# Value blocks split by ScalarE and TensorE, and twelve tiles' moments moved into the first attention part, in a two-layer gated cross-attention kernel

## The reference, cut to what matters

```python
x = x + tanh(g_xattn[0]) * L0_xattn(layernorm(x), ctx, ...)   # the change is in and before this layer
x = x + tanh(g_ffn[0])   * L0_ffn(layernorm(x), ...)          # 4-bit blocks of 16
x = x + tanh(g_xattn[1]) * L1_xattn(layernorm(x), ctx, ...)
x = x + tanh(g_ffn[1])   * L1_ffn(layernorm(x), ...)          # 8 experts, 2 per token

# inside L0_xattn: 16 heads of 16, 77 context rows per batch
q = (x @ Wq + bq);  k = (y @ Wk + bk);  v = (y @ Wv + bv)
out = softmax(q @ k.T / 4) @ v          # per head
return relu(out @ W1 + b1) @ W2 + b2
```

## Time and profile before

| what | value |
|---|---|
| median of 3 runs | 754.19 us (751.41 to 754.39) |
| the profiled execution, its own time | 754.52 us |
| its span, first to last instruction | 752.8 us |
| PE, DVE, ACT, POOL busy, share of the span | 79%, 73%, 47%, 33% |
| first stage, up to barrier 1 | 0 to about 46 us: DVE 36.4 of 47 us busy, PE 22.6 |
| first attention part | about 46 to 147 us: PE 92.4 of 99 us busy, DVE 78.3, POOL 69.5, ACT 64.6 |

### The profile page before, as it was taken

One profiled execution on the slowest core, in us unless ns is written; L12 is line 12 of the kernel. 1 busy time (PEld: TensorE's weight loads), 2 busy tenths in 40 slices (PEclk: granted clock), 3 DMA queues, 4 the chain that ended last, 5 costly groups with the idle time before them and its releaser, 6 DMA issues. The chain is left out here.

```text
span 752.8 us, 15996 instructions
## 1 busy us (share of the span) xinstructions
PE 595.1 (79%) x5555; PEld 531.4 (71%) x5555; DVE 550.4 (73%) x1173; ACT 351.3 (47%) x873; POOL 250.6 (33%) x253
## 2 busy tenths in 40 slices
PE   4559999799524888888885699998681899999950
PEld 3239999699522777777784599997581689999940
DVE  5958898568996699999974478887558675545437
ACT  2256776523125444444432565655255455565620
POOL 2436777700200000000001266666200475555520
PEclk9999999989955899999997899999755899999985
DMA  8020000030000000000000000000195122222229
GB/s 230 2 64 1 3 2 3 2 116 0 1 0 0 1 1 0 0 0 0 0 0 1 1 2 2 2 3 2 40 374 202 50 84 79 78 77 77 68 75 303
DMA packets 27631, 36.66 MB, mean 49 GB/s; under 512 B 4024, under 2 KB 22265, under 8 KB 27438
## 3 DMA queue, kind: packets, MB, share of 16 engines
q1 hardware_dynamic: 23822, 25.56, 10.5%
q0 software_dynamic: 3744, 10.23, 4.3%
HBM read 26.47 MB, written 9.31 MB: 48 GB/s over the span
## 5 line engine op out<-in xcount | busy, mean ns | idle before, releaser
L948 POOL TENSOR_TENSOR rstd<-mv,eps_col 128x16 f32<-128x16 f32 (+2 forms) x6 | 1.3, 210 | 277.6 <-DVE mv L472 277.6
L978 POOL TENSOR_TENSOR p_lo<-prob,p_hi 128x616 f16<-128x616 f32 x64 | 87.2, 1362 | 5.1
L972 POOL CAST p_hi<-prob 128x616 f16<-128x616 f32 x64 | 44.6, 697 | 68.5 <-ACT prob L1101 68.5
L1029 POOL DMA_INDIRECT y_rows<-rn,dst_row x39 | 43.2, 1108 | 54.4 <-DVE rn L897 53.1
L1101 ACT ACTIVATE prob<-prob 128x616 f32<-128x616 f32 x64 | 46.0, 718 | 32.4 <-DVE prob L575 32.3
L1109 ACT ACTIVATE pT<-ps 128x512 f32<-128x512 f32 (+1 forms) x96 | 46.8, 522 | 26.9 <-PE ps L1440 26.5
L575 DVE TENSOR_TENSOR prob<-ps,smax 128x308 f32<-128x308 f32 x128 | 55.3, 474 | 2.2
L1025 POOL DMA_INDIRECT xin<-x_rows,src_row x39 | 38.3, 982 | 52.6 <-DVE dst_row L864 41.0
L461 DVE CAST ehT_hi<-ehid 128x512 fp32r<-128x512 f32 x39 | 16.6, 426 | 52.9 <-ACT ehid L1331 52.8
L570 DVE TENSOR_REDUCE smax<-ps 128x8 f32<-128x616 f32 x64 | 50.6, 790 | 0.2 <-PE ps L1356 0.2
L1354 PE MATMUL ps<-wgu_hi,fxT_hi 128*128 128x352 f32 x128 | 45.0, 352 | 7.1 <-ACT fxT_lo L1215 7.1
(11 more groups left out here) (282 smaller groups left out, 2037.8 us busy)
## 6 DMA issues: line engine op xcount, KB each, us to landing
el_w<-in_L_ffn_W_dram SPq DMA_DIRECT2D x16, 512.0 KB, 9.9
eh_w<-y_rows SPq DMA_DIRECT2D x16, 256.0 KB, 6.0
x_sb<-in_x_dram SPq DMA_DIRECT2D x4, 512.0 KB, 8.5
x_rows<-rn SPq DMA_DIRECT2D x4, 512.0 KB, 9.8
out_dram<-x_sb SPq DMA_DIRECT2D x16, 128.0 KB, 3.5
stage<-in_L_xattn_W_dram SPq DMA_DIRECT2D x2, 512.0 KB, 3.9
eb<-in_L_ffn_b_dram SPq DMA_DIRECT2D x1, 1024.0 KB, 10.3
w<-in_L_ffn_w_down_dram SPq DMA_DIRECT2D x1, 704.0 KB, 7.5
```

Source lines behind the costliest of these rows:

```text
L972: pool.tensor_copy(p_hi[:, t % 2, c], prob[:, t % 2, c]).then_inc(s["hi"], 1)
L978: pool.tensor_tensor(p_lo[:, t % 2, c], prob[:, t % 2, c], p_hi[:, t % 2, c], ALU.subtract).then_inc(s["lo"], 1)
L1029: pool.indirect_dma_start(y_rows, bass.IndirectOffsetOnAxis(ap=dst_row[:, j:j + 1], axis=0), ey[:, j % YRING], None) .then_inc(y_out[j % Y ...
```

## The change

In the first stage the four value blocks are no longer split by DVE. ACT copies the block from PSUM to 16 bits, PE subtracts that copy from the block where it stands in PSUM (a matmul with a negative 16-bit identity `less_h`, without starting a new sum), ACT copies the rest to 16 bits, PE subtracts again, ACT makes the third part. ACT does the first part of all four blocks, then the high parts of the three weight matrices, then the second and third parts. Three of the four small constants are loaded behind the keys' data, the fourth is gone; three semaphores of x become one. POOL waits for both halves of layer 1's keys before it spreads them, and takes over two of the three low weight parts.

Only tiles 0 to 3 have their moments taken in the first stage. DVE takes those of tiles 4 to 7, 8 to 11 and 12 to 15, with their aggregation, at the end of its steps -2, 1 and 5 of the first attention part. POOL makes inverse deviations and shifts of four tiles at a time (`early_rows`): group 0 in the first stage, group 1 ahead of the MLP's first weight, groups 2 and 3 inside `both_halves` at the top of t = 1 and t = 5. ACT's `normalise` of each pair waits for its group.

```diff
+SOON = 4
+LATER = (-2, 1, 5)
@@ SP
-            sp.dma_start(ident[:, :], I["c_ident"]).then_inc(ld["const"], 16)
-            sp.dma_start(head_mask[:, :, :], I["c_head"]...).then_inc(ld["const"], 16)
-            sp.dma_start(k_mask[:, :], I["c_kmask"]).then_inc(ld["const"], 16)
-            sp.dma_start(stage_sel[:, :], I["c_sel"]).then_inc(ld["const"], 16)
             sp.dma_start(ctxT[:, :, :], ...).then_inc(ld["ctx"], 16)
...
             sp.dma_start(bk_col[:, :], I["L0_xattn_bk_cols"]).then_inc(ld["k"], 16)
+            sp.dma_start(k_mask[:, :], I["c_kmask"]).then_inc(ld["const"], 16)
+            sp.dma_start(ident[:, :], I["c_ident"]).then_inc(ld["const"], 16)
+            sp.dma_start(head_mask[:, :, :], I["c_head"]...).then_inc(ld["const"], 16)
...
-                sp.dma_start(x_sb[:, 4 * c:4 * c + 4], ...).then_inc(ld[f"x{c}"], 16)
+                sp.dma_start(x_sb[:, 4 * c:4 * c + 4], ...).then_inc(ld["x1" if c else "x0"], 16)
@@ DVE, first stage
-            for n in range(2):
-                for b in range(B):
-                    g = 2 * n + b
-                    dve.wait_ge(kp["v_ready"], g + 1)
-                    v = ps[0:M, V_BANK[g], 0:D]
-                    ch.link(dve.tensor_copy(v3[:, g, 0], v))
-                    ch.link(dve.tensor_tensor(v_rest[:, 0], v, v3[:, g, 0], ALU.subtract))
-                    ch.link(dve.tensor_copy(v3[:, g, 1], v_rest[:, 0]))
-                    ch.link(dve.tensor_tensor(v_rest[:, 1], v_rest[:, 0], v3[:, g, 1], ALU.subtract))
-                    dve.tensor_copy(v3[:, g, 2], v_rest[:, 1]).then_inc(kp["v3_ready"], 1)
...
-                    if at < TILES:
-                        if at % 4 == 0:
-                            dve.wait_ge(ld[f"x{at // 4}"], 16)
+                    if at < SOON:
+                        if at == 0:
+                            dve.wait_ge(ld["x0"], 16)
                         moments(at)
-                    elif at == TILES:
-                        aggregate(0)
+                    elif at == SOON:
+                        aggregate(0, last=SOON)
...
-            for n, (hi, lo, at) in enumerate(splits):
-                dve.wait_ge(act_done, n + 1)
-                ch.done(dve.tensor_tensor(lo, stage[:, at], two_parts(hi), ALU.subtract))
+            hi, lo, at = splits[0]
+            dve.wait_ge(act_done, 1)
+            ch.done(dve.tensor_tensor(lo, stage[:, at], two_parts(hi), ALU.subtract))
@@ DVE, attention
                     step(k)
...
+                    if n == 0 and k in LATER:
+                        g = LATER.index(k) + 1
+                        dve.wait_ge(ld["x1"], 48)
+                        for t in range(SOON * g, SOON * (g + 1)):
+                            moments(t)
+                        aggregate(0, first=SOON * g, last=SOON * (g + 1))
@@ POOL
+            def shift_rows(k, n, part, first=0, last=TILES):
...
+            def early_rows(g):
+                inverse_deviation(0, g + 1, first=SOON * g, last=SOON * (g + 1))
+                shift_rows(0, 0, 2 * g + 1, first=SOON * g, last=SOON * (g + 1))
+
+            pool.wait_ge(kp["kT_ready"], 2)
             for hf in range(2):
-                pool.wait_ge(kp["kT_ready"], hf + 1)
                 for b in range(B):
                     for hi in (True, False):
                         spread_keys(pool, 1, hf, b, hi)
-            inverse_deviation(0)
-            shift_rows(0, 0, 1)
+            early_rows(0)
+            for n, (hi, lo, at) in enumerate(splits):
+                if n:
+                    pool.wait_ge(act_done, n + 1)
+                    pool.tensor_tensor(lo, stage[:, at], two_parts(hi), ALU.subtract)
             barrier(pool, 1)
...
             def both_halves(n):
                 for t in range(TILES):
+                    if n == 0 and t in (1, 5):
+                        early_rows(2 + t // 5)
                     if t:
                         low_half(n, t - 1, 1)
                     high_half(n, t, 0)
...
+            early_rows(1)
             mlp_weights(0, w1_hi, w1_lo)
@@ ACT
+            act.wait_ge(ld["const"], 48)
+            act.activation(ident_h[:, :], ident[:, :], ACT.Copy)
+            act.activation(neg_ident[:, :], ident[:, :], ACT.Copy, scale=-1.0)
+            act.activation(less_h[:, :], ident[:, :], ACT.Copy, scale=-1.0).then_inc(kp["less"], 1)
             act.wait_ge(ld["v"], 64)
             act.activation(spread[:, :], ...).then_inc(kp["spread"], 1)
+            for g in range(2 * B):
+                act.wait_ge(kp["v_ready"], g + 1)
+                act.activation(v3[:, g, 0], ps[0:M, V_BANK[g], 0:D], ACT.Copy).then_inc(kp["cast"], 1)
             act.wait_ge(ld["q"], 64)
             for hi, _, at in splits:
                 act.activation(hi, stage[:, at], ACT.Copy).then_inc(act_done, 1)
-            act.wait_ge(ld["const"], 64)
-            act.activation(ident_h[:, :], ident[:, :], ACT.Copy)
-            act.activation(neg_ident[:, :], ident[:, :], ACT.Copy, scale=-1.0)
+            for part in range(1, 3):
+                for g in range(2 * B):
+                    act.wait_ge(kp["rest"], 2 * B * (part - 1) + g + 1)
+                    act.activation(v3[:, g, part], ps[0:M, V_BANK[g], 0:D], ACT.Copy)\
+                        .then_inc(kp["cast"] if part == 1 else kp["v3_ready"], 1)
...
                 def normalise(p):
                     att_wait(act, n, "xt", p)
+                    if n == 0:
+                        act.wait_ge(rs[0], 2 * (2 * p // SOON + 1))
...
-                act.wait_ge(rs[2 * n], 2 + n)
+                if n:
+                    act.wait_ge(rs[2], 3)
@@ PE, behind the value matmuls
+            pe.wait_ge(kp["less"], 1)
+            for part in range(2):
+                for g in range(2 * B):
+                    pe.wait_ge(kp["cast"], 2 * B * part + g + 1)
+                    pe.matmul(ps[0:M, V_BANK[g], 0:D], less_h[0:M, 0:M], v3[:, g, part], start=False, stop=True, skip_group_check=True)\
+                        .then_inc(kp["rest"], 1)
```

More of the change, by code:

```diff
@@ L298, in build @@
         ld = {n: sem(f"ld_{n}") for n in
-              "const x0 x1 x2 x3 ctx k v q w1 w2 bias gu up d wg rank eb".split()}
+              "const x0 x1 ctx k v q w1 w2 bias gu up d wg rank eb".split()}
         stored = sem("stored")
@@ L307, in build @@
         dve_done, pool_done, act_done = sem("dve_done"), sem("pool_done"), sem("act_done")
-        kp = sems("kp", "k_ready k_used kT_ready v_ready b_ready b_used v3_ready c_ready c_used zero spread")
+        kp = sems("kp", "k_ready k_used kT_ready v_ready b_ready b_used v3_ready c_ready c_used zero spread less cast rest")
         tanh_ready = sem("tanh_ready")
@@ L327, in build @@
         rt = sems("r", "const xn xt full logit logits_out gates prob both rank spread picked rows meta")
-        mo = sems("e", "hi weights low xt xhi xlo up h ht bias relu split down y acc")
+        mo = sems("e", "hi weights xt xhi xlo up h ht bias relu split down y acc")
         block = ctx.enter_context(nc.Block())
@@ L394, in _ @@
             for c in range(4):
-                sp.dma_start(x_sb[:, 4 * c:4 * c + 4], xt[:, 4 * c:4 * c + 4]).then_inc(ld[f"x{c}"], 16)
+                sp.dma_start(x_sb[:, 4 * c:4 * c + 4], xt[:, 4 * c:4 * c + 4]).then_inc(ld["x1" if c else "x0"], 16)
             sp.dma_start(gates[:, 0:2], I["g_xattn"].rearrange("(a n) -> a n", a=1).broadcast_to([P, 2])).then_inc(ld["bias"], 16)
@@ L949, in inverse_deviation @@
                 pool.tensor_tensor(r, r, eps_col[:, TILES + first:TILES + last], ALU.pow).then_inc(rs[n], 1)
-            pool.wait_ge(ld["const"], 64)
+            pool.wait_ge(ld["const"], 48)
+            def shift_rows(k, n, part, first=0, last=TILES):
+                pool.wait_ge(rs[n], part)
+                ch.link(pool.tensor_tensor(shift_a[:, k, first:last], mv[:, n, first:last, 0], rstd[:, n, first:last], ALU.mult))
+                pool.tensor_scalar(shift_a[:, k, first:last], shift_a[:, k, first:last], -1.0, None, ALU.mult).then_inc(rs[n], 1)
+            def early_rows(g):
+                inverse_deviation(0, g + 1, first=SOON * g, last=SOON * (g + 1))
+                shift_rows(0, 0, 2 * g + 1, first=SOON * g, last=SOON * (g + 1))
+            pool.wait_ge(kp["kT_ready"], 2)
             for hf in range(2):
-                pool.wait_ge(kp["kT_ready"], hf + 1)
                 for b in range(B):
@@ L956, in _ @@
                         spread_keys(pool, 1, hf, b, hi)
-            def shift_rows(k, n, part):
-                pool.wait_ge(rs[n], part)
-                ch.link(pool.tensor_tensor(shift_a[:, k], mv[:, n, :, 0], rstd[:, n], ALU.mult))
-                pool.tensor_scalar(shift_a[:, k], shift_a[:, k], -1.0, None, ALU.mult).then_inc(rs[n], 1)
-            inverse_deviation(0)
-            shift_rows(0, 0, 1)
+            early_rows(0)
[3 more added lines that the diff above has]
+                    pool.tensor_tensor(lo, stage[:, at], two_parts(hi), ALU.subtract)
```

7 lines of the change are left out of this document (3 added, 4 removed).

## The result

The change makes the kernel **slower by 4.9 us**: the median of 13 runs is 757.83 us (755.79 to 762.20) against 752.91 for 13 runs of before (751.41 to 755.82), a ratio of 1.0062 with a 95% interval of 1.0040 to 1.0085. The forecast of 763 us had the direction right and was 5 us too high; the time lies inside the range, near its low end. The profiled execution took 756.03 us, its span is 754.1.

The account below looks back on a forecast made before the run. Engine handoffs (PE, DVE, ACT, POOL) were taken to bound the first stage, PE attention; -6.8 first stage, +5.8 and +6.0 waits, +3.6 clock make +8.6 us on 754.52, so 763 us, range 757 to 767.

Parts of the forecast that it names:

- first stage: Up to barrier 1: earlier loads, new value split and shorter DVE tail together gain 6.8 us, bounds 4.7 and 7.3.
- first wait (tile 0): Attention, top of t = 1: POOL holds for group 2 ahead of tile 0's second low half; PE loses 5.8 us.
- first restart (0 to 1): After PE's pause at tile 0, some 3.5 us run at half-pace clock; 1.8 us lost.
- second wait (3 to 4): Attention, t = 5: POOL holds for group 3 ahead of tile 4's low half; PE loses 6.0 us.
- second restart (4 to 5): After PE's pause at tile 4, some 3.5 us run at half-pace clock; 1.8 us lost.
- the value split: First stage: eight later ACT copies at 0.28 us each, PE's subtractions hidden; slots start at 26.65 instead of 31.86, loads' shift included.
- DVE's tail: End of first stage: two of DVE's three weight subtractions leave, an estimated 0.6 us each, 1.2 us in all.
- rival B: Attention: PE has headroom and wins back 3.8 us of the loss, giving 759.0 us; chance 0.10.
- A: Attention, t = 1 and t = 5: POOL's waits cost PE nothing, only the first stage counts, 747.4 us; chance 0.05.
- C: Attention: the clock does not fall when PE restarts after its pauses; +5.0 us, 759.2 us; chance 0.15.
- D: Attention: one of the two waits, say the second, is covered after all; +0.8 us, 755.0 us; chance 0.08.
- E: First stage: ACT and PE hand each value block back and forth bare; gain falls to 2.9, 766.7 us; chance 0.10.

Follow-up runs that it names:

- the kernel with all sixteen: The changed kernel with all 16 moments back in the first stage and none in attention; median 744.03 us, ratio 0.9863 to the kernel before.

## Why the prediction was right in direction and too high

Its terms against the profiled pair and against the means of the table (three profiles of before, five of after). Waits and restarts are read from the low-part transposes, counted from barrier 1: the shift of tile 0's, then the growth of the steps from tile 0 to 1, 3 to 4 and 4 to 5.

| term | predicted | profiled pair | means |
|---|---|---|---|
| first stage | -6.8 | -8.27 | -8.56 |
| first wait (tile 0) | +5.8 | +4.49 | +5.70 |
| first restart (0 to 1) | +1.8 | +1.18 | +1.47 |
| second wait (3 to 4) | +6.0 | +5.84 | +5.84 |
| second restart (4 to 5) | +1.8 | +1.20 | +1.47 |
| sum at barrier 2 | +8.6 | +4.46 | +5.92 |
| everything behind it | 0 | -3.2 | -1.85 |

**The step that failed is the size of the first stage's gain**: 6.8 us, "bounds 4.7 and 7.3", measured 8.3 to 8.9 between any two profiles of the table and so outside its own bounds. Piece by piece in the profiled pair: the loads gave 2.06 (1.83 predicted; 2.36 by the means), the value split 3.66 (3.4: value blocks' end to slots 7.85, now 4.19), DVE's tail 1.22 (1.2), barrier 1's release behind the last engine 0.46 (0.4). The 0.87 left are in the slots, which took 10.20 us from PE's first to DVE's last eviction (36.08 + 0.26 = 36.34) instead of 11.07 (to 41.79 + 1.14 = 42.93):

```profile
33.10 0.34 PE L1389 MATMUL ps<-v,spread 77*128 77x96 bf16 x2 [0.66 <-DVE vbd_flat L532]
...
41.79 1.14 DVE L532 TENSOR_TENSOR vbd_flat<-ps,head_mask 128x144 bf16<-128x144 f32 x4
```

```profile
28.79 0.38 PE L1413 MATMUL ps<-v,spread 77*128 77x96 bf16 x2 [0.20 <-ACT vbd_flat L1081]
...
36.08 0.26 DVE L522 TENSOR_TENSOR vbd_flat<-ps,head_mask 80x96 bf16<-80x96 f32 x1 [0.40 <-PE ps L1413]
```

The step gave the slots' pace to ACT: "The slots keep ACT's 0.54 each, so the fewer moments on DVE (0.41 each) save nothing there." In the kernel before it was DVE that worked without a gap, from the value split to 45.57, and PE's slots waited for its evictions (the first pair of lines); after the change they wait for ACT's (the second). For the moments between evictions the sentence holds to 0.2 us, as the kernel with all sixteen showed. But DVE in the kernel before had this ahead of its first eviction:

```profile
31.72 0.86 DVE L517 CAST vbd_flat<-head_mask 128x12 bf16<-128x12 f32 x10
32.47 0.42 DVE L466 BATCH_NORM_STATS2 bn<-x_sb 128x6 f32<-128x256 f32 x1
32.81 0.24 DVE L532 TENSOR_TENSOR vbd_flat<-ps,head_mask 128x96 bf16<-128x96 f32 x1
```

The slots started at 31.86, so the first eviction came 0.95 us after them, and now comes 26.44 - 26.14 = 0.30 after: 0.65 of the 0.87, since with the value split gone from DVE the casts and the first moment run in its idle time. The kernel with all sixteen bears it out: with the same moments as before its slots took 10.44 us (26.10 to 36.54), 0.63 less. The prediction followed DVE's queue from the first slot on and not from the end of the value split.

**The two waits** came as forecast, in place, cause and price: the first 5.70 on average, the second 5.84. That the profiled pair has 4.49 for the first goes with the late full pace in that profile of before (tile 0 at 19.55, in the other two at 17.74 and 18.75); the second starts from a steady state, and its pause was 5.68 us in every one of the five profiles. A group's 1.78 us on DVE and 1.88 on POOL, together 0.24 less than put in, and the second wait came out 0.16 below its price.

**The clock** fell at both restarts, at 0.7 of the price: 1.47 instead of 1.8 on average. The term took 3.5 us at half pace; the profile has 3 us at 0.56, which loses 3 x 0.44 = 1.3. The size differs between executions: 1.2 in the first and fifth profiles, 2.3 at tile 0 in the second. That dummy matmuls remove it, with the granted clock at 1.00, shows that it is the clock and not a queue that refills.

**Behind barrier 2** the forecast had no term. The profiles of after are 1.85 us shorter there on average, those of before vary by 2.2 us among themselves, and so by as much as what would have to be explained. Whether a part of it belongs to the change stays open; two kernels with the changed first stage, the one with the rows moved and the one with all sixteen moments, took 603.3 and 603.0 us there, as long as any of before (602.6). The end-to-end 4.9 us lie between 4.1, the mean difference of the spans, and the 5.9 at barrier 2. So the sum of +8.6 missed those 4.1 by 4.5 us: 1.8 in the first stage, 0.3 in the waits, 0.7 in the restarts, and 1.85 behind barrier 2, where it had put nothing.

That 757.83 still lies in the range is luck in part. The low end came out at 758.2 and was put at 757 for a third of rival B, and B is false.

**The rivals.** A (the waits cost PE nothing): false, two pauses. B (headroom): false. PE's weight loads were 9.54 of 10 us busy between the waits as before, and behind the step with the restart a tile takes what it took: 4.99 and 5.98 us in turn, before 4.98 and 5.99. By the rule that the prediction weighed (the Trainium skill, Perfetto Trace Analysis, Identifying the Most-Contended Engine) the share that weight loads leave free would be room, and some of the loss would have come back; nothing did, so 9.54 of 10 left no room here. C (no clock loss): false by the stretch at 0.56. Its 759.2 is nearer to the measured time than the forecast, but for another reason. D (one wait covered): false, both stand in every profile, and moving one group removed one of them. E (copies bare): false, the slots started at 26.14 and not after 29.

## What to carry to other kernels

On an engine that takes its instructions in order, a small job put ahead of a due one costs not only its own length but also the wait for its input: here 1.9 us of rows on POOL made PE 5.7 and 5.8 us late, though the same moments on DVE cost nothing like it when the rows were made elsewhere. So before moving work into a later stage, look at what stands behind it in each queue that it passes, and put it behind the instruction that the bounding engine asks for next, or into idle time at the stage's start, where the same twelve moments cost nothing. When a gain is summed up, follow each engine from the end of the removed work, not from the first instruction that the stage is named after.

## What the runs showed of the hardware

- The time at which PE reaches full pace in the first attention part differs from execution to execution: 14.6 us after barrier 1 and at the latest 8.7 us after it in two profiles of the kernel before, and the same two values in the fourth and third of the changed kernel. Stretches ahead of that moment show a granted clock of 1.00, but that is no reading: the trace's record of the clock begins only there (at 60.66 us in the first profile of before, where matmuls of 256 columns go from one each 0.21 us to one each 0.12 at 60.67). Before it, only the distance of the matmuls tells.
- The same untouched code of nearly 390 us took 386.0 to 391.2 us in 17 profiles. Two executions can agree closely: in the first and fifth profiles of the changed kernel it took 387.86 in both, with the same granted clock. Part of the length shows in that clock: from 240 to 280 us behind barrier 2 it is 0.83 and then 0.74 (20 us each) in these two, 0.74 and 0.66 in the second of before; but the first of before has 0.79 and 0.78 and is as long as the second. What picks a length is not settled; the start time alone does not.
- Ten casts of 128x12 took 0.86 us when POOL was idle and 4.00 us in all five profiles of the changed kernel (one has 3.99), when POOL was spreading keys beside them. Here that was hidden.
